# Starting 24 of 71 expert blocks early, from a table of their own, and sending six results inside the last dispatch

## The chip, the cores and the metric

One core of one Trainium2 chip. The metric is the device time of one execution in microseconds (us), as the median of several; the profile shows one execution, with times from the start of its span.

## What the kernel computes

The reference is a one-layer model over 8 sequences of 512 tokens, with 192 features per token:

```python
h = tok(x, quantum_params, post_w, post_b)          # 6-qubit circuit per token, then a linear map to 192
h = h + attention(layernorm(h), W_qkv, b_qkv)       # one head, softmax over 512 keys
h = h + experts(layernorm(h), Wg, W1, b1, W2, b2)   # 8 experts, the best 2 per token
```

`experts` takes, for each token, the two experts with the largest gate scores, weighs their outputs (gelu of a 192 to 384 map, then 384 to 192) with a softmax over these two scores, and adds them up.

## The kernel before, in words

A token's features stay in a short form: 32 numbers (the six circuit values, the attention's weights over them, the shares), from which matrices worked out at the start give everything else. The 4096 tokens are 8 batches of 512, each 4 tiles of 128.

**Attention** runs as one pipeline over the batches, with the order of every engine written out by hand. For batch b TensorE (`pe`) makes scores in two orders (`both_scores`), VectorE (`dve`) takes row maxima, ScalarE (`act`) takes the exponentials, and then follow `context`, `merged`, `a_transpose`, `gram`, the choice of two experts (`route_and_root`), the place of each token among those of its expert (`ranks`, `slots`), the features scaled for the experts (`normed`) and the shares (`shares`, which need an exponential that ScalarE takes in `gap_exponent`). `residual` writes what a batch has before its experts into `hres`.

**Dispatch.** GpSimd (`pool`) sends each batch's rows to `routed` in DRAM with eight indirect DMAs (`scatter(b, 0)` and `scatter(b, 1)`, four each, 64 in all). Each expert has its own region of `routed`, in order of tokens.

**Expert blocks.** A block is 128 rows of one expert. There are at most `BLOCKS` = 71 blocks, in `STEPS` = 18 steps of four. `block_table` on VectorE works out, from the counts of all batches, where each block starts in `routed` and which expert's weights it needs (`t_i`). Blocks that hold rows of the first four batches alone come first: their first 24 are called `EARLY`. SyncE (`sp`) loads the 71 blocks one after the other, each with a register load from the table and then a DMA (lines 412 and 413): it first waits for `table_done`, then for the scatters of batches 0 to 3 (`scattered_early`), and before block 24 for those of batches 4 to 7 (`scattered_late`). For each step VectorE copies the up weights of its four blocks (`expert_up`, L1430); TensorE turns the four blocks (`block_transpose`, L1912), multiplies them with the up weights (`up_proj`, L1923) and then multiplies each with its down weights (`down_proj`, L1933, six matmuls); ScalarE takes the gelu (L1612) and multiplies with the share (`weighted`, L1624) into one of `RESULTS` = 8 result buffers. GpSimd sends each result to `shares_out` in DRAM (L696); before it sends result m it waits until result m - 4 has landed.

**End.** For each batch SyncE loads its two sums from `shares_out` (`load_sums`, L418) when enough results have landed: 39 for batches 0 to 3, then 47, 55, 63 and 71. VectorE adds them to `hres` (`add_experts`, L1417), and SyncE stores the batch (L422). SyncE takes load b + 1 before store b, all in one queue, behind the 71 block loads. On VectorE the additions stand in one order with the copies: `expert_up(14)`, additions of batch 0, `expert_up(15)`, batch 1, `expert_up(16)`, batch 2, `expert_up(17)`, batches 3 to 7.

Of the kernel before, what the change touches and what calls it, by code (L numbers as in the profile page):

```python
# [16 lines left out]
QUBITS = 6  # L17
# [14 lines left out]
def build(nc, token_ids, angles, emb_two, emb_raw, qkv_w, gate_w, up_w, down_w, out):  # L32
# [23 lines left out]
    RESULTS = 8  # L56
    LAG = 4
    ADDS_FROM = (2 * HALF * SEQ // P + E) // STEP + 4
# [24 lines left out]
    shares_out = nc.dram_tensor("shares_out", (2 * TOKENS, D), F32, kind="Internal").ap()  # L83
    shares_view = shares_out.rearrange("(k b p j) d -> b p k (j d)", k=2, b=BATCHES, j=TILES)
# [4 lines left out]
    with ctx:  # L89
# [7 lines left out]
        theta_all = sb("theta_all", [P, T, ANGLES])  # L97
        angle_stages = sb("angle_stages", [P, 3, CT, ANGLES])
        turns, turned, folded = [angle_stages[:, i] for i in range(3)]
        sine = sb("sine", [P, 2, USED, CT])  # L100
        cosine = sb("cosine", [P, 2, USED, CT])
# [4 lines left out]
        bloch = table("bloch", QUBITS, 8)  # L106
# [3 lines left out]
        chain = table("chain", QUBITS, 16)  # L110
        chain_q = table("chain_q", 4, 2, 2, 2)
# [55 lines left out]
        own_row = sb("own_row", [P, 2])  # L167
# [10 lines left out]

        def behind(room, pattern, **sizes):
            size = int(np.prod(list(sizes.values())))  # L180
            room[1] += size
            return room[0][:, room[1] - size:room[1]].rearrange(pattern, **sizes)
# [54 lines left out]
        t_i = sb("t_i", [P, 2], I32)  # L237
        xt = sb("xt", [P, 1, P])
# [3 lines left out]
        y = behind(up_room_1, "p (n d) -> p n d", n=RESULTS, d=D)  # L242
        hid = behind(up_room_1, "p (n h) -> p n h", n=STEP, h=HID)
        expert_sums = [prob[:, :, :].rearrange("p j s -> p (j s)")[:, 0:2 * TILES * D].rearrange("p (k x) -> p k x", k=2),
# [88 lines left out]
        count_done = sem("count_done")  # L333
        table_done = sem("table_done")
        block_in = [sem(f"block_in{s}") for s in range(STEPS)]
# [13 lines left out]
        def blocks_of(s):  # L349
            return range(s * STEP, min(s * STEP + STEP, BLOCKS))  # L350

# [39 lines left out]
        def _(sp):  # L391
# [1609 lines left out]
```

## Time and profile before

| | us |
|---|---|
| median of 3 runs (313.16 to 313.82) | 313.63 |
| the profiled execution | 313.38 |
| its span | 311.7 |

The profiled execution is 1.68 us longer than its span; that part lies outside the profile. A row of the timeline gives the start, the length (of several instructions run together, from the first start to the last end), the engine, the line, the operation, what it writes and reads, and in brackets the engine's idle time before it. SPq is the queue in which SyncE issues DMAs; PEld is TensorE's loading of weights. PEclk is the clock granted to TensorE as a share of 2.4 GHz.

### The profile page before, as it was taken

The numbers are of one execution on the slowest core, as the hardware profiler recorded it, in microseconds if no ns is written. First come the engines' busy times: TensorE is split into PE (matmuls) and PEld (weight loads), VectorE is DVE, ScalarE is ACT, GpSimd is POOL, SyncE is SP. The second block draws the span as 40 slices with busy tenths as digits, with TensorE's granted clock in tenths as the row PEclk, the third lists the DMA queues.
The fourth block names the chain that finished last, engine by engine and source line by source line (L and its number), as shares of the span: only waits on it lengthen the run. The fifth ranks groups of instructions, "written<-read, shape, count | busy, mean of one in ns | idle before, by whom it ended". The sixth has DMA issues, their size and how long they took to land.

```text
span 311.7 us, 6161 instructions
## 1 busy us (share of the span) xinstructions
PE 223.4 (72%) x1551; PEld 151.6 (49%) x1551; DVE 176.3 (57%) x685; ACT 119.4 (38%) x283; POOL 209.1 (67%) x281
## 2 busy tenths in 40 slices
PE   0650995587838689776885627999999999999600
PEld 0540652232514335443543226887878888777400
DVE  4756999647899886858468732312222221655222
ACT  1002012426522403564322333655655656555300
POOL 5776975803996878777767773676766765767540
PEclk9999999555885655798555556999999999999955
DMA  7810007970000000000000011222222225798634
GB/s 178 242 20 12 1 7 261 344 291 3 0 0 2 9 9 15 13 16 14 13 13 13 14 30 32 68 92 88 82 81 91 68 84 150 271 331 274 209 84 187
DMA packets 24398, 28.90 MB, mean 93 GB/s; under 512 B 14890, under 2 KB 17825, under 8 KB 24171
## 3 DMA queue, kind: packets, MB, share of 16 engines
q1 hardware_dynamic: 17884, 20.56, 21.2%
q0 software_dynamic: 6480, 7.94, 8.3%
q8 instruction: 14, 0.23, 0.3%
q14 instruction: 20, 0.16, 0.2%
HBM read 13.54 MB, written 15.63 MB: 94 GB/s over the span
## 4 chain that ended last, share of the span: by engine, by line
PE 47%; DVE 23%; POOL 9%; issue 7%; DMA 6%; ACT 5%; SPq 2%; DVEq 0%; POOLq 0%; ACTq 0%
PE bank_b L1933 27%; PE bank_a L1923 5%; POOL theta_all L462 5%; PE bank_b L1736 4%; PE bank_a L1743 3%; DVE nmax L1116 3%; POOL rs L634 2%; PE bank_c L1755 2%; DMA shares_out<-up 2%; ACT prob L1481 2%; DMA angle_stages<-shares_out 2%; PE bank_a L1809 1%; POOL routed L645 1%; SPq L412 1%; DVE chain_q L811 1%
## 5 line engine op out<-in xcount | busy, mean ns | idle before, releaser
L696 POOL DMA_INDIRECT shares_out<-up x71 | 72.6, 1022 | 38.8 <-ACT up L1624 19.4
L1933 PE MATMUL bank_b<-wide,up 128*128 x426 | 85.7, 345 | 2.3 <-issue 1.5
L645 POOL DMA_INDIRECT routed<-rows,slot x64 | 62.4, 975 | 22.6 <-issue 18.8
L1933 PEld LDWEIGHTS bank_b<-wide,up 128*128 128x128 f32 x426 | 68.2, 191 | 16.9 <-issue 16.7
L1430 DVE COPY up<-wide 32x384 f32 x71 | 26.6, 374 | 63.2 <-PE bank_a L1923 35.2
L1624 ACT ACTIVATE up<-bank_b,up 128x192 f32<-128x192 f32 x71 | 29.8, 420 | 35.3 <-PE bank_b L1933 34.5
L462 POOL DMA_INDIRECT theta_all<-angles,ids x32 | 31.2, 976 | 10.8 <-issue 9.0
L1612 ACT ACTIVATE up<-bank_a 128x384 f32<-128x384 f32 x71 | 34.2, 485 | 11.1 <-PE bank_a L1923 10.6
L1743 PE MATMUL bank_a<-keys_t,wt 32*128 32x512 f32 x64 | 27.8, 955 | 4.7 <-DVE nmax L1116 3.0
L1736 PE MATMUL bank_b<-queries_t,keys_t 32*128 32x512 f32 x64 | 24.6, 849 | 6.3 <-ACT keys_t L1459 3.5
L1116 DVE TENSOR_REDUCE nmax<-bank_a 128x2 f32<-128x1024 f32 x16 | 19.5, 1220 | 11.3 <-PE bank_a L1743 11.3
L1481 ACT ACTIVATE prob<-bank_b 128x1024 f32<-128x1024 f32 x16 | 16.4, 1023 | 16.3 <-PE bank_b L1736 16.3
L1923 PE MATMUL bank_a<-xt,up 32*128 32x128 f32 x426 | 18.5, 305 | 0.4 <-ACT xt L1618 0.4
L1809 PE MATMUL bank_a<-m,a2t 32*128 32x192 f32 x64 | 14.0, 523 | 4.8 <-ACT hres L1489 2.7
L1923 PEld LDWEIGHTS bank_a<-xt,up 32*128 32x128 f32 x426 | 15.0, 201 | 4.7 <-issue 4.0
L1755 PE MATMUL bank_c<-prob,u 128*32 128x128 f32 x256 | 12.9, 366 | 0.9 <-ACT prob L1481 0.7
L1809 PEld LDWEIGHTS bank_a<-m,a2t 32*128 32x128 f32 x64 | 7.5, 273 | 11.8 <-issue 10.5
L1447 ACT ACTIVATE sine<-angle_stages 128x480 f32<-128x480 f32 (+2 forms) x3 | 2.4, 784 | 28.2 <-DVE angle_stages L767 28.2
L1417 DVE TENSOR_TENSOR hres<-hres,prob 128x384 f32<-128x384 f32 x12 | 6.2, 554 | 10.8 <-DMA prob<-shares_out 10.7
L1755 PEld LDWEIGHTS bank_c<-prob,u 128*32 128x32 f32 x256 | 9.5, 146 | 5.0 <-ACT prob L1481 2.3
L1489 ACT COPY hres<-bank_a 128x384 f32<-128x384 f32 x16 | 7.6, 477 | 10.6 <-PE bank_a L1809 10.6
L1736 PEld LDWEIGHTS bank_b<-queries_t,keys_t 32*128 32x128 f32 x64 | 7.0, 251 | 9.1 <-issue 7.8
(399 smaller groups left out, 361.5 us busy)
## 6 DMA issues: line engine op xcount, KB each, us to landing
routed<-pad_rows SPq DMA_DIRECT2D x8, 528.0 KB, 5.2
out<-hres SPq DMA_DIRECT2D x8, 384.0 KB
wide<-down_w SPq DMA_DIRECT2D x1, 2304.0 KB, 11.7
prob<-shares_out SPq DMA_DIRECT2D x3, 768.0 KB, 4.8
angle_stages<-shares_out SPq DMA_DIRECT2D x3, 768.0 KB, 6.5
up<-up_w SPq DMA_DIRECT2D x1, 1536.0 KB
form_p<-shares_out SPq DMA_DIRECT2D x2, 768.0 KB
up<-routed SPq DMA_DIRECT2D x71, 16.0 KB, 1.7
```

Source lines behind the costliest of these rows:

```text
L462: pool.indirect_dma_start(out=theta_all[:, t, :], out_offset=None, in_=angles, in_offset=bass.IndirectOffsetOnAxis(ids[:, b, j:j + 1], 0)) ...
L645: pool.indirect_dma_start(out=routed, out_offset=bass.IndirectOffsetOnAxis(slot[:, b, k, j:j + 1], 0), in_=rows[:, b, k, j, :], in_offset=None
L696: pool.indirect_dma_start(out=shares_out, out_offset=bass.IndirectOffsetOnAxis(xb[:, m, DEST:DEST + 1].bitcast(I32), 0), in_=y[:, m % RESU ...
L1116: dve.tensor_reduce(nmax[:, b % 2, 2 * h:2 * h + 2], bank_a[:, 0:2, :], AX.X, ALU.max, negate=True).then_inc(max_done, 1)
L1430: copied = dve.tensor_copy(up_now[r, s % 2, :], wide_flat[r, bass.ds(first + HC * D, HID)])
L1612: act.activation(hid[:, n, :], bank_a[:, n, 0:HID], ACT.Gelu).then_inc(gelu_done, 1)
L1624: act.mul(y[:, m % RESULTS, :], bank_b[:, m % 2, 0:D], xb[:, m, SHARE:SHARE + 1]).then_inc(y_done, 1)
L1736: mm = pe.matmul(bank_b[:, n, :], keys_t[r, bt % 3, k * P:(k + 1) * P], queries_t[r, :], start=True, stop=True)
L1743: mm = pe.matmul(bank_a[:, n, :], wt[r, bs % 2, :], keys_t[r, bs % 3, :], start=True, stop=True)
L1755: mm = pe.matmul(bank_c[j * F:(j + 1) * F, 0:P], u[:, b * TILES + k, :], prob[:, k, j * P:(j + 1) * P], start=(k == 0), stop=(k == TILES - 1),
L1923: mm = pe.matmul(bank_a[:, n, c * P:(c + 1) * P], up_now[r, s % 2, c * P:(c + 1) * P], xt[r, 0, :], start=True, stop=True)
L1933: mm = pe.matmul(bank_b[:, m % 2, 0:D], hid[:, m % STEP, c * P:(c + 1) * P], wide_flat[:, bass.ds(first + c * D, D)], start=(c == 0), stop ...
```

## The change

- **An early table.** With the counts of the first four batches (one more small matmul in `ranks(3)`, one more copy in `slots(3)`) VectorE works out the table of the first 24 blocks by itself (`early_table`, behind the last row maxima). It holds the rows in `routed`, the down weights and the up weights of each block.
- **Up weights by DMA.** SyncE writes all up weights once to `up_rows` in DRAM, long before. For the first 24 blocks (6 steps) it then loads, in addition to each block, that block's up weights from there, with a register load of its own. VectorE copies up weights from step 6 on only.
- **The order on SyncE.** It waits for `early_done` and the early scatters, issues four blocks and four up weights for each of the six steps, and then waits for `table_done` and the late scatters and issues the other 47 blocks.
- **The order on TensorE and ScalarE.** The expert steps start behind the last score products. The rest of the attention stage (`context(7)`, `merged`, `a_transpose`, `gram`, `ranks(6)` and `ranks(7)`) stands between the first expert operations. The residuals of batches 4 to 7 follow in pieces behind blocks 8 to 28, on other banks, and ScalarE copies each half in two pieces. The counts for the whole table move into `ranks(7)`; `block_table` moves ahead of `shares(7)`. The gelu is no longer touched in advance.
- **Results.** 24 result buffers in place of 8 (they lie where the circuit's tables were). GpSimd sends the first six results between `scatter(7, 0)` and `scatter(7, 1)`.

The core of the diff:

```diff
-    RESULTS = 8
+    RESULTS = 24
+    EARLY_STEPS = EARLY // STEP
+    TAIL_FIRST = 2 * STEP
+    TAIL_PIECES = 3 * (BATCHES - HALF) - 1
     LAG = 4
+    AHEAD = 6
...
+            sp.wait_ge(up_copied, E)
+            sp.dma_start(up_rows.rearrange("(e f) h -> f e h", f=F), wide[0:F, :, HC * D:WIDE]).then_inc(up_out, 16)
+
+            def load_up(m):
+                row = sp.value_load(t_early[m:m + 1, 2:3], min_val=0, max_val=(E - 1) * F)
+                n = m % STEP
+                sp.dma_start(up_early[m // STEP][n * F:(n + 1) * F, :], up_rows[bass.ds(row, F), :]
+                             ).then_inc(early_up_in[m // STEP], 16)
+
             def load_block(m):
-                row = sp.value_load(t_i[m:m + 1, 0:1], min_val=0, max_val=ROWS - P)
+                row = sp.value_load(table_of(m)[m:m + 1, 0:1], min_val=0, max_val=ROWS - P)
...
+            sp.wait_ge(early_done, 1)
+            sp.wait_ge(up_out, 16)
+            sp.wait_ge(scattered_early, 16 * 2 * TILES * HALF)
+            for s in range(EARLY_STEPS):
+                for m in blocks_of(s):
+                    load_block(m)
+                for m in blocks_of(s):
+                    load_up(m)
             sp.wait_ge(table_done, 1)
-            sp.wait_ge(scattered_early, 16 * 2 * TILES * HALF)
-            for m in range(EARLY):
-                load_block(m)
             sp.wait_ge(scattered_late, 16 * 2 * TILES * (BATCHES - HALF))
...
+                if b == BATCHES - 1:
+                    for m in range(AHEAD):
+                        result(m)
                 scatter(b, 1)
-            for m in range(BLOCKS):
...
+            for m in range(AHEAD, BLOCKS):
+                result(m)
...
                 normed(i - 2)
+                if i == BATCHES + 1:
+                    block_table()
                 shares(i - 2)
                 if i + 1 < BATCHES:
                     row_max(i + 1, 1)
                     spread_max(i + 1)
-
-            block_table()
+                    early_table()
...
-            for s in range(STEPS):
+            for s in range(EARLY_STEPS, STEPS):
                 expert_up(s)
...
+            xt_copy(0)
+            context_copy(BATCHES - 1)
+            at_copy(BATCHES - 1)
+            gap_exponent(BATCHES - 2)
             for m in range(STEP - 1):
                 gelu(m)
             xt_copy(1)
...
                 if m > 0:
                     weighted(m - 1)
+                    tail_copy(m - 1)
...
+                if m == 2:
+                    gap_exponent(BATCHES - 1)
...
-            residual(BATCHES - 1, 0)
-            residual(BATCHES - 1, 1)
-            pe.wait_ge(table_done, 1)
+            pe.wait_ge(early_done, 1)
             pe.wait_ge(down_in, 16)
-            pe.wait_ge(h2_copied, 2 * BATCHES)
             block_transpose(0)
+            context(BATCHES - 1)
             up_proj(0)
+            merged(BATCHES - 1)
+            a_transpose(BATCHES - 1)
+            ranks(BATCHES - 2)
+            gram(BATCHES - 1)
             block_transpose(1)
             for m in range(BLOCKS):
                 s, n = divmod(m, STEP)
+                if m == EARLY:
+                    pe.wait_ge(table_done, 1)
                 down_proj(m)
                 if n == 0 and s + 1 < STEPS:
                     up_proj(s + 1)
+                if m == 1:
+                    ranks(BATCHES - 1)
                 if n == 2 and s + 2 < STEPS:
                     block_transpose(s + 2)
+                tail(m)
```

## Rows read from the trace of the kernel before

**Rows 1.** The page's chain that ended last, shares of the span by engine
```profile
PE 47%; DVE 23%; POOL 9%; issue 7%; DMA 6%; ACT 5%; SPq 2%; DVEq 0%; POOLq 0%; ACTq 0%
```

**Rows 2.** Stretches of 4 us: busy time by engine, granted clock, DMA share
```profile
core 0: us, PE busy (x) PEld busy (x) DVE busy (x) ACT busy (x) POOL busy (x), PEclk, DMA share, GB/s
148.00:152.00 4.00, 4.00 (x42) 3.07 (x44) 2.84 (x26) 1.03 (x3) 3.06 (x4) 0.50 0.05 12
152.00:156.00 4.00, 2.82 (x17) 1.48 (x15) 0.96 (x7) 1.95 (x4) 2.88 (x3) 0.50 0.07 16
...
188.00:192.00 4.00, 3.24 (x15) 2.51 (x19) 0.74 (x3) 1.08 (x3) 0.91 (x1) 0.50 0.13 23
192.00:196.00 4.00, 4.00 (x42) 3.75 (x35) 1.05 (x3) 1.99 (x6) 1.45 (x2) 0.87 0.16 40
```

**Rows 3.** Timeline of SyncE's queue, from the first block load to the end
```profile
178.54 82.33 SPq L413 DMA_DIRECT2D up<-routed  x71
260.99 0.39 SPq L418 DMA_DIRECT2D prob<-shares_out  x1
...
301.50 0.36 SPq L418 DMA_DIRECT2D angle_stages<-shares_out  x1
```

**Rows 4.** Median time of a DMA from issue to landing
```profile
up<-routed SPq DMA_DIRECT2D x71, 16.0 KB, 1.7
...
routed<-rows,slot POOLq DMA_INDIRECT x64, 2.1
```

**Rows 5.** Timeline of VectorE, end of the row maxima, start and end of `block_table`
```profile
147.59 0.18 DVE L1123 COPY w_rep<-nmax 128x16 f32<-128x16 f32 x1
...
173.69 0.16 DVE L1357 CAST count_i<-bank_a 128x8 int32<-128x8 f32 x1
...
177.40 0.16 DVE L1393 TENSOR_TENSOR t_i<-t_sum,own_row 128x2 int32<-128x2 f32 x1
```

**Rows 6.** Timeline of GpSimd: dispatch, first and last results
```profile
145.69 0.95 POOL L645 DMA_INDIRECT routed<-rows,slot  x1 [0.30 <-issue]
...
179.07 0.96 POOL L645 DMA_INDIRECT routed<-rows,slot  x1 [0.31 <-issue]
...
187.94 0.97 POOL L645 DMA_INDIRECT routed<-rows,slot  x1 [0.30 <-issue]
192.78 1.00 POOL L696 DMA_INDIRECT shares_out<-up  x1 [3.88 <-ACT up L1624]
...
298.05 0.98 POOL L696 DMA_INDIRECT shares_out<-up  x1 [0.31 <-DMA shares_out<-up]
299.33 0.98 POOL L696 DMA_INDIRECT shares_out<-up  x1 [0.30 <-issue]
```

**Rows 7.** Timeline of TensorE: first expert operations, `block_transpose(6)`, `up_proj(15)`, last blocks
```profile
189.24 2.29 PE L1933 MATMUL bank_b<-wide,up 128*128 x6 [0.47 <-issue]
191.45 1.67 PE L1923 MATMUL bank_a<-xt,up 32*128 32x128 f32 x24
...
217.88 0.27 PE L1912 MATMUL bank_d<-ident,up 128*128 128x128 f32 x1
...
272.66 0.95 PE L1923 MATMUL bank_a<-xt,up 32*128 32x128 f32 x24
...
286.19 7.01 PE L1933 MATMUL bank_b<-wide,up 128*128 x36
```

**Rows 8.** Timeline of VectorE: additions of batch 0, then the copies of step 15
```profile
265.83 2.09 DVE L1417 TENSOR_TENSOR hres<-hres,prob 128x384 f32<-128x384 f32 x4 [6.43 <-DMA prob<-shares_out]
...
270.23 0.46 DVE L1430 COPY up<-wide 32x384 f32 x1 [0.73 <-issue]
```

**Rows 9.** Timeline of ScalarE: the table for the gelu, and the last result
```profile
179.36 1.28 ACT L1629 ACT_TABLE_LOAD   x1
...
293.23 0.42 ACT L1624 ACTIVATE up<-bank_b,up 128x192 f32<-128x192 f32 x1 [0.73 <-PE bank_b L1933]
```

**Rows 10.** TensorE's matmuls of the residuals, by line
```profile
L1809 PE MATMUL bank_a<-m,a2t x64: 320/522/685, 122.4 to 178.3; 32*128 32x192 f32 x64
```

More of the change, by code:

```diff
@@ L109, in build @@
         step_m = table("step_m", QUBITS - 2, 8)
-        chain = table("chain", QUBITS, 16)
-        chain_q = table("chain_q", 4, 2, 2, 2)
+        chain = circuit_table(QUBITS, 16)
+        chain_q = circuit_table(4, 2, 2, 2)
         ends = table("ends", 6)
@@ L332, in build @@
         h2_out = sem("h2_out")
-        count_done = sem("count_done")
         table_done = sem("table_done")
+        early_done = sem("early_done")
+        up_out = sem("up_out")
+        early_up_in = [sem(f"early_up_in{s}") for s in range(EARLY_STEPS)]
         block_in = [sem(f"block_in{s}") for s in range(STEPS)]
@@ L350, in blocks_of, with table_of, tail_piece, tail_issued @@
             return range(s * STEP, min(s * STEP + STEP, BLOCKS))
+        def table_of(m):
+            return t_early if m < EARLY else t_i
+        def tail_piece(m):
+            k = 2 * ((m - TAIL_FIRST) // STEP) + m % STEP
+            return k + 1 if m >= TAIL_FIRST and m % STEP < 2 and k < TAIL_PIECES else None
+        def tail_issued(m):
+            done = [tail_piece(n) for n in range(m) if tail_piece(n) is not None]
+            turned = HALF + 1 + len([k for k in done if k % 3 == 0])
+            return turned, 2 * HALF + len(done) - (turned - HALF - 1)
         def blocks_until(b):
@@ L648, in scatter, with all_landed, result @@
                         ).then_inc(scattered_early if b < HALF else scattered_late, 16)
+            def all_landed(m):
+                pool.wait_ge(added[m % RESULTS], 16 * (m // RESULTS + 1))
+                pool.sem_inc(landed, 1)
+            def result(m):
+                pool.wait_ge(y_done, m + 1)
+                if m >= LAG:
+                    all_landed(m - LAG)
+                pool.indirect_dma_start(
+                    out=shares_out, out_offset=bass.IndirectOffsetOnAxis(xb[:, m, DEST:DEST + 1].bitcast(I32), 0),
+                    in_=y[:, m % RESULTS, :], in_offset=None, bounds_check=2 * TOKENS - 1,
+                    oob_is_err=False).then_inc(added[m % RESULTS], 16)
             def constants():
@@ L1810, in residual, with late_a2_transpose, late_residual, tail @@
                 mm.then_inc(h2_done, 1)
-            def counts():
-                pe.wait_ge(max_done, 2 * BATCHES)
-                for n, b in enumerate(ENDS):
-                    mm = pe.matmul(bank_a[:, 0, n * E:(n + 1) * E], ones_b[:, :], both[:, b, TILES, :], start=True,
-                                   stop=True)
-                mm.then_inc(count_done, 1)
+            def late_a2_transpose(b, m):
+                pe.wait_ge(gates_done, b + 1)
+                pe.wait_ge(xt_copied, m // STEP + 2)
+                pe.wait_ge(h2_copied, 2 * b)
+                pe.transpose(bank_d[:, 0:P], flat(ev, b), ident[:, :]).then_inc(a2t_done, 1)
+            def late_residual(b, h, m):
+                pe.wait_ge(table_done, 1)
+                pe.wait_ge(a2t_copied, b + 1)
+                pe.wait_ge(xt_copied, m // STEP + 2)
+                pe.wait_ge(h2_copied, 2 * b + h)
+                for n in range(2):
+                    r = slice((2 * h + n) * F, (2 * h + n + 1) * F)
+                    into = bank_c[:, 0:D] if n else bank_d[:, P:P + D]
+                    mm = pe.matmul(into, a2t[r, :], m2[r, :], start=True, stop=True)
+                mm.then_inc(h2_done, 1)
+            def tail(m):
+                k = tail_piece(m)
+                if k is not None:
+                    b, part = HALF + k // 3, k % 3
+                    if part == 0:
+                        late_a2_transpose(b, m)
+                    else:
+                        late_residual(b, part - 1, m)
             pe.wait_ge(weights_done, 3)
@@ L1875, in _ @@
             a2_transpose(1)
[L1877 to L1881 removed]
+            for i in range(LAST[0] + 1, BATCHES):
+                queries(i)
+                context(i - 1)
                 residual(i - 4, 0)
```

191 lines of the change are left out of this document (123 added, 68 removed).

## The prediction, made before the changed kernel was run

> **What bounds the kernel now.** I read the chain that ended last first: TensorE holds 47% of it, more than any other engine [rows 1]. Then the timelines from the middle to the end. The expert stage begins when the table is there: `block_table` ends at 177.56, and SyncE's first block load follows at 178.54 [rows 3, 5]. TensorE starts its first down product at 189.24 and its last ones end at 286.19 + 7.01 = 293.20 [rows 7]; in between it goes from step to step with nothing that waits for loads, since the last of the 71 loads is out by 260.87, 32 us ahead of its use [rows 3, 7]. GpSimd ends its dispatch at 187.94 + 0.97 = 188.91, waits 3.88 us for the first result and issues the last one at 299.33 [rows 6]. The end hangs on that: the last sum is loaded at 301.50, and 10.2 us later the span is over [rows 3]. So three runs stand beside each other: SyncE (71 loads, 178.54 to 260.87), TensorE (189 to 293) and GpSimd (120 to 300). An earlier start helps only as far as all three come along.
>
> **SyncE's queue, before and after.** Its loads come at (82.33 - 0.34) / 70 = 1.17 us from start to start, where 0.34 is about one DMA's own issue; the rest is the register load [rows 3]. No row shows a load of up weights, but it is the same pair, a register load and a DMA; I take 1.16, as in the early part, and bound it below by 1.11 (the pace of the first loads, my reading of the same timeline) and above by 1.5.
> - Start: the row maxima end at 147.77 [rows 5]. `early_table` has ten small operations; `block_table` has seventeen in 3.87 us, 0.23 each [rows 5]. So 147.77 + 2.3 = 150.1, and the first load 0.98 later (177.56 to 178.54), at 151.1. The early scatters are no hindrance: the 32nd of 64 is issued at 145.69 and lands 2.1 later [rows 4, 6].
> - The early stage: 48 loads, 151.1 + 48 x 1.16 = 206.8. Step s has its up weights at 151.1 + (8s + 7) x 1.16 + 1.7: step 0 at 160.9, step 5 at 207.3 (landing 1.7 [rows 4]). TensorE gets a step every 9.3 us.
> - The late 47 loads: the last starts at 206.8 + 46 x 1.17 = 260.6, and the first sum can be loaded at 261.1. Before it was 260.99. **The start moves 27.4 us forward, and the 24 added loads take 24 x 1.16 = 27.8 us of the same queue: for SyncE the early start is worth nothing.** What the change can save must come from the last 50.7 us, where before SyncE waited for results.
>
> **TensorE.** The parts of the attention stage that it now does between the first expert operations are moved, not removed; their cost lies under the 9.3 us per step, in which a step at full clock needs about 5.8 (from `block_transpose(6)` at 217.88 to `up_proj(15)` at 272.66 are 9.4 steps, 54.8 us [rows 7]). What holds TensorE is block 24: the load of block 27, step 6's last, is issued at 206.8 + 3 x 1.17 = 210.3 and landed at 212.0. So `block_transpose(6)` comes at 212.0 instead of 217.88: **5.9 us earlier, not 28**. From there on it runs as before. Behind blocks 20 to 28 stand four residual halves of two matmuls, 0.32 us at their shortest, and one transpose [rows 10]: 1.6 us by estimate, bounded by 0 (hidden behind weight loads) and 4. `up_proj(15)` would come at 212.0 + 54.8 + 1.6 = 268.4.
>
> **VectorE's order adds a wait.** `expert_up(15)` stands behind the additions of batch 0, and these wait for the first sum: 4.84 us after its issue before (260.99 to 265.83), and the four copies behind them end at 270.69 [rows 3, 8]. With the first sum at 261.1 they end at 270.8, so `up_proj(15)` waits 2.4 us, to 270.9. Behind it are step 16's and 17's copies, each behind one more addition of 2.09; they come in time. From `up_proj(15)` to the last product was 293.20 - 272.66 = 20.5; I take 20.0, since 16 more result buffers spare TensorE the short waits for a free one. End of TensorE: 290.9 instead of 293.2.
>
> **GpSimd.** A scatter takes (187.94 - 179.07) / 7 = 1.27 us, a result 1.28 [rows 6]. `scatter(7, 0)` is due at 179.07 and needs `shares(7)`, which now stands behind `block_table` (3.87) and behind `ranks(7)`, which TensorE reaches only after `down_proj(1)`. At half clock that is 160.9 + about 13.5 (gelu's table 1.28 [rows 9], three products of 2.3 and 1.7 [rows 7], and the rest of the attention) = 174.5; with 2.9 for slots, features and shares, 181.2. So GpSimd stalls 3 us. Then four scatters, six results (7.7) and four scatters: 199.9. The late scatters land at 202, before SyncE asks for them at 206.8, so this delay costs nothing; if the loads came faster it would. The floor of the other 65 results is 199.9 + 65 x 1.28 = 283.1, under TensorE's 290.9, so the six early results are not on the path either: GpSimd does the same 135 DMAs and catches up with TensorE.
>
> **The sum.** Last product 290.9, its share 0.42 [rows 9], last result issued by 291.5, last sum 2.17 later as before (299.33 to 301.50), at 293.7, and 10.2 to the end: 303.9. The gain is mostly the backlog of GpSimd: before it issued its last result 6.1 us after TensorE's last product, held up by the landing of results while the sums were loaded. With more buffers the backlog can lie longer, so I keep some of it, and some DMA time: 304 for the span, which with the 1.68 outside gives 305.7, from a profiled execution of 313.38 (0.25 below the median, which I neglect). **I forecast 305.5 us**, own range 301 to 309.
>
> **Rivals.**
> - *The loads come faster than 1.16.* The Trainium skill ("DMA: Bandwidth & Descriptors", Issuing engines are not separate DMA queues) says that the sequencer's time to initiate a DMA is usually small beside the DMA. Here rows 3 and 4 say otherwise, 1.17 against 1.7 us. By that rule the queue would hardly count. As a mechanism of this kernel: at 1.11 the late loads start at 204.4, `block_transpose(6)` comes at 209.5, the first sum at 256.5; TensorE ends some 4.5 earlier, 299.5 for the span, 301 us. Its floor is GpSimd's: 283.1 + 1.28 + 2.17 + 10.2 = 296.7 for the span, 298.4 us. Chance 0.20.
> - *Landing takes over.* From 261 the loads of sums run without a wait for results, beside 19 results, each of which waits for the fourth before it. If these go at 2.0 us apiece, as against 1.28 undisturbed, the last is issued at 261.1 + 19 x 2.0 = 299.1; 311.5 for the span at worst, half of that excess more likely, 308 to 311 us. Chance 0.15.
> - *No change: a load of up weights is dearer.* At 1.5 us (24 x 0.34 = 8.2 more) the first sum and block 24 come 8.2 later and all the gain is gone, 313.5 us. Nothing in the profile speaks for it but that no row shows it. Chance 0.07.
> - *Slower: TensorE at half clock.* The granted clock is 0.50 from 148 to 192, through a stretch in which TensorE is busy 2.82 of 4 us, and even through one of 4.00; it is up only in the stretch of 192 to 196, in the unbroken run that starts at 189.24 [rows 2, 7]. The early stage has gaps, a step every 9.3 us. The skill ("TensorE: Matmul & The Clock Gate", Part 1: The HAM clock gate) states that the throttled clock is the default and activity releases it; the trace agrees with it. If the clock stayed at half through the six early steps, a down product would take 2.29, an up projection 1.67 and a transpose about 0.5 [rows 7]. From 168.2, where the first product starts, nineteen, five and five of them end at 222.6, 10.6 after the 212.0 above, and five more products lose another 5.7; less the wait of 2.4 that this swallows, the end moves by 13.9, to some 319 us. It decides from a delay of about 10 us over the six steps on. Against it: at 4 x 2.29 + 1.67 + 0.5 = 11.3 per step of 9.3 TensorE would have no gap left, and an unbroken run is what brought the clock up. Chance 0.08.
>
> **How the numbers follow.** Forecast 0.50, faster loads 0.20, landing 0.15, dearer loads 0.07, half clock 0.08. A measurement of this kernel can tell about 0.2%, 0.6 us, from no change. Faster: 0.50 + 0.20 + 0.15 = 0.85; same 0.03 and slower 0.04 share the dearer loads; slower with the clock 0.12. The range of 298 to 312 takes in the first three cases and leaves out the last two and a little.
>
> **What would show it.** SyncE: 48 loads from about 151, the last of 95 near 260.6, the first sum near 261. TensorE: `up_proj(0)` near 161, steps 9.3 us apart until `block_transpose(6)` at 212, steps of 5.8 behind it, a wait before `up_proj(15)`. GpSimd: a stall of 3 us before `scatter(7, 0)`, six results, the dispatch over at 200, and its last result within 1 or 2 us of TensorE's last product. It would be wrong if the loads of up weights kept another pace than the blocks', if the clock fell in the early stage and TensorE got behind its loads, or if results and sums hindered each other more than before.

## The result, and the profile after

The changed kernel takes 310.74 us (median of 20 runs, 307.78 to 314.07), the kernel before 312.86 us on the same chip (20 runs, 309.77 to 315.40). The ratio is 0.9933 with a 95% interval of 0.9904 to 0.9961: 0.7% faster, where the forecast was 305.5 us, 2.6% faster, with an own range of 301 to 309. Medians here are of all runs and ratios of those within about 1.5% of their kernel's fastest, so that a ratio is not always the quotient of two medians. The profiled execution took 310.14 us, its span is 308.1 us.

The page's chain that ended last, shares by engine, to be set against [rows 1]:

```profile
SPq 27%; DVE 22%; PE 15%; issue 13%; POOL 9%; DMA 7%; ACT 5%; DVEq 1%; POOLq 0%; ACTq 0%
```

TensorE has lost the chain (15% against 47%), SyncE's queue has it. The timeline of that queue, from the first block load on, answers to [rows 3]:

```profile
150.81 4.05 SPq L458 DMA_DIRECT2D up<-routed  x4
155.63 3.59 SPq L453 DMA_DIRECT2D up<-up_rows  x4
160.41 3.71 SPq L458 DMA_DIRECT2D up<-routed  x4
...
200.90 3.65 SPq L453 DMA_DIRECT2D circuit<-up_rows  x4
205.39 54.13 SPq L458 DMA_DIRECT2D up<-routed  x47
259.64 0.39 SPq L463 DMA_DIRECT2D prob<-shares_out  x1
...
298.17 0.36 SPq L463 DMA_DIRECT2D angle_stages<-shares_out  x1
```

It starts 27.7 us earlier and loads its first sum 1.4 us earlier (259.64 against 260.99). TensorE, against [rows 7]; the two transposes are those of steps 6 and 7:

```profile
160.78 1.67 PE L2058 MATMUL bank_a<-xt,up 32*128 32x128 f32 x24
...
210.76 0.33 PE L2037 MATMUL bank_d<-ident,up 128*128 128x128 f32 x1
...
218.03 0.27 PE L2037 MATMUL bank_d<-ident,up 128*128 128x128 f32 x1
...
269.62 0.95 PE L2058 MATMUL bank_a<-xt,up 32*128 32x128 f32 x24 [0.36 <-DVE up L1515]
...
283.76 7.22 PE L2070 MATMUL bank_b<-wide,up 128*128 x36 [0.60 <-ACT up L1693]
```

The last product ends at 290.98 (293.20 before). GpSimd, against [rows 6]: the stall ahead of the last batch's first scatter, the dispatch's end, and the last results.

```profile
180.53 0.96 POOL L695 DMA_INDIRECT routed<-rows,slot  x1 [1.67 <-issue]
...
197.16 0.95 POOL L695 DMA_INDIRECT routed<-rows,slot  x1 [0.31 <-issue]
...
286.34 0.98 POOL L708 DMA_INDIRECT shares_out<-circuit,up  x1 [1.25 <-ACT circuit L1705]
289.32 1.37 POOL L708 DMA_INDIRECT shares_out<-circuit,up  x1 [2.00 <-ACT circuit L1705]
291.00 0.98 POOL L708 DMA_INDIRECT shares_out<-circuit,up  x1 [0.30 <-issue]
292.29 0.98 POOL L708 DMA_INDIRECT shares_out<-circuit,up  x1 [0.30 <-issue]
293.58 0.98 POOL L708 DMA_INDIRECT shares_out<-circuit,up  x1 [0.30 <-issue]
296.02 0.98 POOL L708 DMA_INDIRECT shares_out<-circuit,up  x1 [1.46 <-issue]
```

The last result leaves 5.0 us behind the last product (6.1 before). The end of the chain, in order of time (start, length, what), says what held it:

```profile
288.72 0.43 ACT circuit L1705
289.32 3.95 DMA shares_out<-circuit,up
293.58 0.98 POOL shares_out L708
294.56 0.72 issue
295.31 0.71 issue
296.02 2.08 DMA shares_out<-circuit,up
298.17 5.01 DMA angle_stages<-shares_out
```

The row to see is the second: a result's own transfer stands in the chain ahead of later results. GpSimd, before it issues result m, waits until result m - 4 has landed. The result of 289.32 is the fifth from the end, and the view of its tile gives it 5.9 us from issue to landing, not only the 3.95 of the chain; it landed at 295.2, and the last result, which waits for it, left at 296.02. The timeline names ScalarE for the waits at 286.34 and 289.32. For the first this is right: ScalarE ended that result at 285.46, 0.88 before, and 0.88 is also the distance at other waits for ScalarE (at 249.16, for instance). For the second it is not: ScalarE had ended at 286.62, 2.70 before, and the landing came last. So the profiled span of 308.1 divides at the last product: 291.0 up to it, 17.1 behind it. Before it was 293.2 and 18.5.

### The profile page after: what moved, and what is told of

Its sections match the earlier page's. It is cut to its first block, busy times and chain, and to the rows that moved or that the text cites. A ratio compares the mean times of both kernels' runs of the same rounds, so it can differ in the third digit from the quotient of the medians.

```text
span 308.1 us, 6215 instructions
## 1 busy us (share of the span) xinstructions
PE 220.3 (72%) x1552; PEld 150.4 (49%) x1552; DVE 170.0 (55%) x675; ACT 121.3 (39%) x292; POOL 208.2 (68%) x281
## 4 chain that ended last, share of the span: by engine, by line
SPq 27%; DVE 22%; PE 15%; issue 13%; POOL 9%; DMA 7%; ACT 5%; DVEq 1%; POOLq 0%; ACTq 0%
SPq L457 11%; SPq L458 10%; PE bank_b L2070 5%; POOL circuit L512 5%; SPq L451 4%; PE bank_a L1835 3%; DVE nmax L1175 3%; SPq L453 3%; PE bank_b L1828 2%; POOL rs L684 2%; DMA shares_out<-circuit,up 2%; DMA angle_stages<-shares_out 2%; DMA prob<-shares_out 2%; POOL routed L695 1%; ACT prob L1566 1%
## 5 line engine op out<-in xcount | busy, mean ns | idle before, releaser
L708 POOL DMA_INDIRECT shares_out<-circuit,up x71 | 71.5, 1007 | 35.1 <-issue 17.3
L2070 PE MATMUL bank_b<-wide,up 128*128 x426 | 88.4, 350 | 6.0 <-ACT up L1693 1.8
L2070 PEld LDWEIGHTS bank_b<-wide,up 128*128 128x128 f32 x426 | 69.7, 195 | 22.1 <-issue 22.0
L1515 DVE COPY up<-wide 32x384 f32 x47 | 18.3, 389 | 65.9 <-PE bank_a L2058 49.7
L1705 ACT ACTIVATE circuit<-bank_b,up 128x192 f32<-128x192 f32 x71 | 29.9, 421 | 38.2 <-PE bank_b L2070 38.2
L512 POOL DMA_INDIRECT circuit<-angles,ids x32 | 31.2, 976 | 10.8 <-issue 9.0
L1532 ACT ACTIVATE circuit<-angle_stages 128x480 f32<-128x480 f32 (+2 forms) x3 | 2.3, 781 | 28.2 <-DVE angle_stages L823 28.2
L1502 DVE TENSOR_TENSOR hres<-hres,angle_stages 128x384 f32<-128x384 f32 x12 | 6.2, 555 | 8.5 <-DMA angle_stages<-shares_out 8.4
L1835 PEld LDWEIGHTS bank_a<-keys_t,wt 32*128 32x128 f32 x64 | 7.0, 261 | 7.4 <-issue 4.8
L1540 ACT COPY wide<-bank_a 128x384 f32<-128x384 f32 x8 | 3.8, 478 | 16.7 <-PE bank_a L1773 16.7
```

The source lines that it names most:

```text
L512: pool.indirect_dma_start(out=theta_all[:, t, :], out_offset=None, in_=angles, in_offset=bass.IndirectOffsetOnAxis(ids[:, b, j:j + 1], 0)) ...
L708: pool.indirect_dma_start(out=shares_out, out_offset=bass.IndirectOffsetOnAxis(xb[:, m, DEST:DEST + 1].bitcast(I32), 0), in_=y[:, m % RESU ...
L1705: act.mul(y[:, m % RESULTS, :], bank_b[:, m % 2, 0:D], xb[:, m, SHARE:SHARE + 1]).then_inc(y_done, 1)
L1835: mm = pe.matmul(bank_a[:, n, :], wt[r, bs % 2, :], keys_t[r, bs % 3, :], start=True, stop=True)
L2070: mm = pe.matmul(bank_b[:, m % 2, 0:D], hid[:, m % STEP, c * P:(c + 1) * P], wide_flat[:, bass.ds(first + c * D, D)], start=(c == 0), stop ...
```

## The experiments

Each kernel was timed several times in turn with the kernel before on the same chip, and a ratio is to those runs; the kernel that loads its sums last was run once. Ratios of different groups of runs compare less well than those of one group. The edits are to the changed kernel, but for one to the kernel before; cuts in them are marked with three dots. The "tail" is the time from the end of TensorE's last product to the end of the span.

**The six early results back behind the dispatch.**
```
-    AHEAD = 6
+    AHEAD = 0
```


> The first six results go behind the dispatch, as before; all else as in the changed kernel. First theory (the six early results are not on the path): the dispatch ends 7.7 us earlier, near 190.5, GpSimd still does the same 135 DMAs, TensorE's last product stays near 291 and the span within 1 us of 308.1. Rival (sending them early is what pays): the span grows by 3 us or more.

Measured: 312.05 us, ratio 0.9965 (0.9918 to 1.0011). In its profile the dispatch is over at 190.8, the first sum is loaded at 260.66, the last result leaves at 296.42: neither of these two moves by more than 1.1 us, and the span is 308.5. TensorE's last product, expected near 291, came at 292.86; the tail was shorter by 1.5. At the pace of this kernel the six results are not on the path.

**Twelve results between a result and the landing it waits for, instead of four.**
```
-    LAG = 4
+    LAG = 12
```


> GpSimd waits for the landing of result m - 12 instead of m - 4 before it sends result m. First theory (the last results are held by the landing of the fourth before them, 6.5 us each while sums are loaded): the last result is issued within 1.5 us of TensorE's last product, at about 292 instead of 296, the last sum is loaded at about 296 and the span is about 305 to 306. Rival (the DMA engines are full, so that results only queue there instead of on GpSimd): the last result is issued earlier but lands as late as before, last sum at 298 and span 307.5 to 308.5.

Measured: 313.55 us, ratio 1.0048 (1.0013 to 1.0084); the simple remedy fell. The last result did leave 1.3 us behind the last product (296.57 against 293.99 + 1.24). But GpSimd's wait is also the report on which SyncE loads sums, and it now comes eight results later:

```profile
296.69 0.36 SPq L463 DMA_DIRECT2D prob<-shares_out  x1
...
302.79 0.36 SPq L463 DMA_DIRECT2D angle_stages<-shares_out  x1
```

The sum before the last is loaded at 296.69, beside the last results, and these land late again: 302.79 for the last sum, 6.2 us behind the last result (2.2 in the changed kernel). The last sum and the span of 312.7 lie outside what either theory expected.

**No sum loaded before all 71 results have landed.** The additions stand behind all copies of VectorE.
```
-                sp.wait_ge(landed, blocks_until(b))
+                sp.wait_ge(landed, BLOCKS)
-    ADDS_FROM = (2 * HALF * SEQ // P + E) // STEP + 4
+    ADDS_FROM = STEPS
```


> No sum is loaded before all 71 results have landed, and the additions stand behind all copies of up weights. The whole is slower by the unhidden sums; the place of the last result is what counts. First theory (sums loaded beside results hold the results up): each result lands in about 2.4 us to the end, and the last one is issued within 1.5 us of the last product, near 291 to 292. Rival (results are late for another reason, a wait on ScalarE or the pace of GpSimd itself): the last result stays 4 to 5 us behind the last product.

The time, 332.29 us, is that of eight sums one after the other and says nothing; the stretch of the results does. TensorE's last products, GpSimd's last result and, under them, the median landing of results from 255 to 293:

```profile
282.99 6.93 PE L2070 MATMUL bank_b<-wide,up 128*128 x36
```
```profile
292.02 0.99 POOL L708 DMA_INDIRECT shares_out<-circuit,up  x1 [0.30 <-issue]
```
```profile
shares_out<-circuit,up POOLq DMA_INDIRECT x27, 2.3
```

The same for the changed kernel, from 255 to 310:

```profile
form_p<-shares_out SPq DMA_DIRECT2D x2, 768.0 KB, 6.9
shares_out<-circuit,up POOLq DMA_INDIRECT x26, 4.0
```

Without sums in flight a result lands in 2.3 us, and the last one leaves 2.1 us behind the last product (282.99 + 6.93 = 289.92); with them it takes 4.0 and the last one leaves 5.0 behind. So the sums' loads, and the stores of finished batches (384 KB each) that go with them, cost 2.9 us there, through GpSimd's wait. The 2.1 is more than the 1.5 that the first theory allowed, but far from the rival's 4 to 5.

**SyncE spared twelve register loads and DMAs.** VectorE copies the up weights of steps 3 to 5, as it does those of the later steps.
```
+    LOADED_UPS = 3
-                for m in blocks_of(s):
+                for m in blocks_of(s) if s < LOADED_UPS else ():
                     load_up(m)
...
-            for s in range(EARLY_STEPS, STEPS):
+            for s in range(LOADED_UPS, STEPS):
                 expert_up(s)
...
```


> Only steps 0 to 2 have their up weights loaded by SyncE; VectorE copies those of steps 3 to 5 from the full weights, behind shares(7), where it was idle. SyncE has 12 loads less. First theory (the loads of up weights take from SyncE's queue what the early start gives): the early stage is over on SyncE near 192, the late loads start when the late scatters have landed, near 199.5 instead of 205.4, the first sum comes near 253.5 instead of 259.6, TensorE's block_transpose(6) near 205, its last product some 4 to 5 us earlier, and the span some 4 us shorter, 304, or less if the end is held by landings. Rival (what bounds is behind SyncE: landing of results and sums): the first sum moves by 6 us, but the last result and the end by less than 1.

Measured: 304.93 us, ratio 0.9764 (0.9708 to 0.9820). The first sum is loaded at 256.34, the last product ends at 289.66. That is 1.3 us earlier for TensorE, not the 4 to 5 expected; the profiled span (304.6) is 3.5 shorter, and the other 2.2 lie in the tail (14.9). That the gain stops short of the theory's 253.5 for the first sum is seen in TensorE's row of step 6:

```profile
206.81 0.33 PE L2039 MATMUL bank_d<-ident,up 128*128 128x128 f32 x1 [2.41 <-DMA up<-routed]
207.66 3.66 PE L2071 MATMUL bank_b<-wide,up 128*128 x12 [0.52 <-issue]
```

It waits for a block whose rows the last scatter brings, and that one is issued at 198.07, behind the six results. Now they are on the path. The 3.66 us for twelve products, 2.37 in the changed kernel, is the lower clock: the granted clock is 0.57 from 208 to 212.

**The same with the six results behind the dispatch.** The diffs of the first and the fourth kernel together.

> The run with SyncE's loads of steps 3 to 5 given to VectorE, with the six results behind the dispatch again. Theory (with the short queue the dispatch ends later than SyncE, so the six results now cost): the late scatters land some 7 us sooner, SyncE's late run starts at about 171 to 173 us instead of 178.4, block_transpose(6) comes at about 203 without a wait and without the half clock behind it, the first sum is issued at 248 to 251, the span is 299 to 302 and the ratio to the run with the six ahead some 0.98 to 0.99. Rival (the end is held by the results' landing): TensorE gains up to 4 us, the last result still leaves over 2 us behind the last product, and the span stays within 1.5 us of 304.6.

Measured: 304.19 us, ratio 0.9718 (0.9673 to 0.9762). The dispatch ends at 189.1, step 6 starts at 203.68 without a wait, the first sum is loaded at 245.83, the last product ends at 283.00: TensorE gains 6.7 us on the kernel above, some 2 of them because step 6 keeps the full clock (6.6 us for the step, 8.6 above).

```profile
245.83 0.50 SPq L464 DMA_DIRECT2D prob<-shares_out  x1
```

The span gains 3.9, since the tail takes the rest: 17.7 us against 14.9. The ratios of the two kernels can't be told apart. Both theories had a part of it. The chain's end has the transfers of results in it again:

```profile
276.74 3.15 DMA shares_out<-circuit,up
...
280.61 4.85 DMA shares_out<-circuit,up
```

**GpSimd waits for no landing.** ScalarE waits for the transfer from its own buffer, SyncE for those of the sums that it loads.
```
-                if m >= LAG:
-                    all_landed(m - LAG)
...
-                    act.wait_ge(landed, m - RESULTS + 1)
+                    act.wait_ge(added[m % RESULTS], 16 * (m // RESULTS))
...
-                sp.wait_ge(landed, blocks_until(b))
+                done = blocks_until(b)
+                for m in range(max(done - RESULTS, blocks_until(b - 1) if b else 0), done):
+                    sp.wait_ge(added[m % RESULTS], 16 * (m // RESULTS + 1))
```


> The changed kernel, in which GpSimd waits for no landing: ScalarE (before it writes a result's buffer again) and SyncE (before it loads sums) wait for the results' transfers themselves. Theory (GpSimd's wait for the landing of the result four before paces the end): the results leave as they are made, the last one within 2.5 us of the last product (5.0 in the changed kernel), the last sum is loaded at 294 to 296 instead of 298.2, the span falls by 2 to 4 us, ratio to the kernel before 0.981 to 0.988. Rival (the transfers themselves are slow beside the loads of the sums, and whoever waits for them waits as long): the last result may leave earlier, but the last sum is loaded at 297 to 299 and the span stays at 307.5 to 308.5.

Measured: 309.75 us, ratio 0.9872 (0.9819 to 0.9924). The last result leaves 1.8 us behind the last product (293.35 + 1.24 = 294.59), as the theory says:

```profile
293.35 1.24 PE L2068 MATMUL bank_b<-wide,up 128*128 x6 [0.20 <-issue]
```
```profile
296.34 0.98 POOL L708 DMA_INDIRECT shares_out<-circuit,up  x1 [0.30 <-issue]
```

But the last product is 3.6 us later than in the changed kernel. So the last sum (298.57) and the span (308.4) are where the rival put them; from the last product to the last sum it is 4.0 us, against 7.2 in the changed kernel, as in the theory. Two things are seen ahead of the late product. The first sum is loaded 0.85 us behind the last block load (206.71 + 55.26 = 261.97, then 262.82), where the changed kernel has 0.12: SyncE now goes through 24 semaphores there. And step 6 runs in part at the lower clock (below).

**The residual pieces on three blocks of a step instead of two.**
```
-            k = 2 * ((m - TAIL_FIRST) // STEP) + m % STEP
-            return k + 1 if m >= TAIL_FIRST and m % STEP < 2 and k < TAIL_PIECES else None
+            k = 3 * ((m - TAIL_FIRST) // STEP) + min(m % STEP, 2)
+            return k + 1 if m >= TAIL_FIRST and m % STEP != 2 and k < TAIL_PIECES else None
...
```


> The changed kernel with the eleven residual pieces on three blocks of each step instead of two, so that the last is done with block 21 instead of block 28. Theory (the pieces lengthen the steps behind block 12, 6.3 to 6.9 us against 5.76, and this carries to the end): the last product comes 1 to 2 us earlier and the ratio falls by 0.003 to 0.006. Rival (the end is set by SyncE's first sum at 259.6, the additions and the copies behind it): TensorE is earlier in steps 9 and 10 only, waits that much longer at up_proj(15), and the last product stays within 0.5 us of 291.0.

Measured: 310.46 us, ratio 0.9908 (0.9871 to 0.9944), not to be told from the changed kernel. TensorE is 0.9 us earlier in step 14 and waits 0.92 instead of 0.36 at `up_proj(15)`; its last product ends at 290.84. The rival holds: the pieces are not what sets the end.

**All four parts: copies by VectorE, six results behind, pieces moved, no landing waited for by GpSimd.**

> The parts together: up weights of steps 3 to 5 copied by VectorE, the six results behind the dispatch, the pieces on three blocks of a step, and no wait for a landing on GpSimd. Theory (SyncE's queue, then the late scatters, then the landing of the results are the gates in this order): first sum at 247 to 251, last product at 283 to 287, last result within 2.5 us of it, span 295 to 300, ratio to the kernel before 0.945 to 0.96. Rival (another gate, VectorE with 24 copies more or the transfers of the sums, holds the end): the span stays at 302 to 304.6.

Measured: 300.45 us, ratio 0.9594 (0.9543 to 0.9645), span 298.5; the last product ends at 284.44, the last result leaves 1.9 us behind it.

**The same without the pieces.**

> Up weights of steps 3 to 5 copied by VectorE, the six results behind the dispatch, and no wait for a landing on GpSimd; the residual pieces as in the changed kernel. Theory (GpSimd's wait for the landing of the result four before holds the last results up, the pieces hardly count): last product at 282.5 to 284, last result within 2.5 us of it (5.4 with the wait), ratio to the kernel before 0.958 to 0.966, as with the pieces moved (0.9594). Rival (the pieces gave that gain): ratio 0.968 to 0.974, as with the wait (0.9718).

Measured: 301.16 us, ratio 0.9694 (0.9626 to 0.9761), span 297.3; last product 283.18, last result 2.0 behind it. By the profile the theory holds. The ratio lies in the rival's bounds (0.968 to 0.974) and not in the theory's (0.958 to 0.966), but its interval covers both, so it cannot decide on the pieces.

**The kernel before, with no landing waited for by GpSimd.** The same edit in the kernel before; its eight buffers stay.

> The kernel before, in which GpSimd waits for no landing: ScalarE and SyncE wait for the results' transfers themselves; its eight result buffers stay. Theory (the tail behind the last product is GpSimd's wait for the landing of the result four before, in the kernel before as in the changed one): the last result leaves within 2.5 us of the last product instead of 6.1, span 307.5 to 309.5, ratio 0.986 to 0.993; the change then keeps no more of its gain than TensorE's 2.2 us. Rival (with eight buffers whoever waits for them waits as long): ScalarE waits for its buffer, the last product moves to 294 to 297, the span stays within 1 us of 311.7.

Measured: 310.19 us, ratio 0.9954 (0.9910 to 0.9998), span 306.9. The last result leaves 1.6 us behind the last product (285.19 + 7.29 = 292.48) instead of 6.1:

```profile
285.19 7.29 PE L1931 MATMUL bank_b<-wide,up 128*128 x36 [0.25 <-issue]
```
```profile
294.12 1.35 POOL L696 DMA_INDIRECT shares_out<-up  x1 [0.30 <-issue]
```

So the backlog is not the change's: the kernel before had it already. The gain in time is smaller than expected (0.986 to 0.993) and than the span of the one profile promised.

**The changed kernel with both, no landing on GpSimd and the pieces moved.**

> The changed kernel, with no wait for a landing on GpSimd and the residual pieces on three blocks of a step. Theory (the profile with the direct waits alone was late in TensorE by a stretch at the lower clock, which is not in the edit): last product at 290 to 292, last result within 2.5 us of it, span 303.5 to 306, ratio to the kernel before 0.980 to 0.986. Rival (without the wait on GpSimd the results crowd the DMA engines sooner and TensorE gets its blocks later): last product at 293 to 295 again, span 307 to 308.5, ratio 0.986 to 0.992.

Measured: 309.21 us, ratio 0.9910 (0.9870 to 0.9950), span 305.8. Last product 291.90, last result 1.5 behind it; the span is where the theory put it; the ratio is in the rival's bounds (0.986 to 0.992), and not below that of the moved pieces with the wait (0.9908, another group of runs). SyncE's 24 semaphores cost 0.85 here too (205.93 + 54.42 = 260.35, then 261.20).

**Additions one step further back in VectorE's order.**
```
-    ADDS_FROM = (2 * HALF * SEQ // P + E) // STEP + 4
+    ADDS_FROM = (2 * HALF * SEQ // P + E) // STEP + 5
```


> The changed kernel with the additions of each batch one step further back in VectorE's order, so that the copies for up_proj(15) no longer stand behind those of batch 0. Theory (this order costs the 0.4 us that the profile shows before up_proj(15), not the 2.4 of the forecast): last product at 290.3 to 291.2, the span within 1.5 us of 308.1, ratio 0.991 to 0.998. Rival (the wait only shows as short since TensorE was late itself): the last product comes 1.5 to 2.5 us earlier and the ratio falls to 0.985 to 0.990.

Measured: 310.32 us, ratio 0.9965 (0.9924 to 1.0005), span 308.4, last product 292.29. Nothing is gained, so the order of additions and copies cost no 2.4 us. The last product missed the theory's 290.3 to 291.2 by 1.1; step 6 came 0.7 later in this execution.

**GpSimd waits for no landing in its last twelve results alone; SyncE for the last sixteen results itself, and the changed kernel beside it.**
```
-                if m >= LAG:
+                if LAG <= m < REPORTED + LAG:
                     all_landed(m - LAG)
...
-                sp.wait_ge(landed, blocks_until(b))
+                sp.wait_ge(landed, min(blocks_until(b), REPORTED))
+                for m in range(max(blocks_until(b - 1), REPORTED) if b else BLOCKS, blocks_until(b)):
+                    sp.wait_ge(added[m % RESULTS], 16 * (m // RESULTS + 1))
...
```
Here REPORTED is 55.

> The changed kernel, in which GpSimd waits for no landing in its last twelve results alone; SyncE waits for the last sixteen results itself, before the last two sums. Theory (the tail is GpSimd's wait, and the version with direct waits throughout lost part of what it gained to SyncE's 24 waits in front of the first sum, 0.85 us against 0.12): first sum at once behind the late loads, last product at 290 to 291.5, last result within 2.5 us of it, from the last product to the end of the span 13.8 to 14.6 (17.1 in the changed kernel), ratio to the kernel before 0.979 to 0.987, 0.007 to 0.011 under that of the changed kernel in the same call. Rival (the transfers hold the end, whoever waits): 16 to 17.5 us from the last product to the end, ratio within 0.004 of the changed kernel's.

> The changed kernel itself, beside the two others on the same chip: ratio to the kernel before 0.990 to 0.996 as on record. By both theories the same.

Measured: 308.20 us, ratio 0.9840 (0.9798 to 0.9881), and for the changed kernel beside it 310.43 us, 0.9899 (0.9854 to 0.9944). The difference, 0.006, is just under the 0.007 to 0.011 expected and past the rival's 0.004, though the two intervals overlap. The last result leaves 1.8 us behind the last product, the tail is 14.6, and the first sum follows 0.11 us behind the last block load. The last product, at 294.18, was 2.7 us later than expected, again with step 6 at the lower clock.

**The same with VectorE's copies and the six results behind the dispatch.**

> The same with the up weights of steps 3 to 5 copied by VectorE and the six results behind the dispatch. Theory: TensorE's last product at 282.5 to 284 as in the runs with these two parts, 13.8 to 14.6 from it to the end, span 296.5 to 298.5, ratio 0.955 to 0.967. Rival (as above): span 299.5 to 301.5, ratio 0.969 to 0.976.

Measured: 301.46 us, ratio 0.9652 (0.9607 to 0.9696), span 299.1, tail 14.4; against the kernel with the same parts and the wait (0.9718) 0.7% less, measured in another group of runs, and the intervals touch. The last product, at 284.67, is 0.7 later than expected, and the span 0.6 longer. This and the two other kernels that join these parts, 300.5 to 301.5 us, are the fastest found and can't be told apart.

From the end of TensorE's last product to the end of the span, worked out from each profile:

| GpSimd waits for result m - 4 to the end | us | does not | us |
|---|---|---|---|
| before | 18.5 | before, no wait | 14.4 |
| changed | 17.1 | changed, no wait | 13.8 |
| VectorE copies, six behind | 17.7 | the same, no wait | 14.1 |
| additions later | 16.1 | changed, none for the last twelve | 14.6 |
| pieces moved | 15.3 | pieces moved, no wait | 13.9 |
| VectorE copies | 14.9 | all four parts | 14.1 |
| six results behind | 15.6 | VectorE copies, six behind, none for the last twelve | 14.4 |

(The kernel that waits for result m - 12 has 17.4.) With the wait the tail varies from 14.9 to 18.5; without it, it is 13.8 to 14.6. That it varies with how the last sums fall among the last results is a reading of the timelines, not a test.

## Why the prediction was wrong

**Right: SyncE's queue.** First load 150.81 (151.1 forecast), late loads from 205.39 (206.8), first sum 259.64 (261.1); the 24 added loads did eat the 27 us of the early start. The kernel with VectorE's copies and the six results behind shows the price: twelve loads less, and its first sum comes 259.64 - 245.83 = 13.8 us earlier, 1.15 a load. With VectorE's copies alone the time is 1.7% less by the two ratios (0.9764 against 0.9933, intervals apart, different groups of runs). The Trainium skill ("DMA: Bandwidth & Descriptors", Issuing engines are not separate DMA queues) calls the time to initiate a DMA usually small beside the DMA. The trace agrees for the issue alone, 0.33 us (median of the block loads) beside 1.7 to the landing. The prediction set 1.17 us against that rule, but most of it is the register load ahead of each DMA, with what goes with it: in the chain the line that loads a block's register, 457, has 11% of the span, the line of the DMA, 458, 10%. So the rule gave the rival "the loads come faster" no support; the pace was 1.14 us in the early part and 1.17 in the late.

**TensorE's end: right by number, in part by luck.** `up_proj(0)` at 160.78 (161), step 6 at 210.76 (212.0), last product 290.98 (290.9). The terms between were mis-sized against each other. Steps 6 to 8 took 7.27, 6.67 and 6.55 us, where later ones take 5.85, 2.9 us for the pieces in all (1.6 forecast). The wait before `up_proj(15)` was 0.36 (2.4). From there to the end it took 290.98 - 269.62 = 21.4 us, not 20.0; before it was 20.5, so the added buffers spared nothing here. The experiments with moved pieces and with later additions show that neither sets the end by itself. The profiled execution was also an early one: in the profiles of two near kernels with the same loads and the wait (six results behind, additions later) the last product came at 292.9 and 292.3. The rival "half clock" did not come: the granted clock, 0.50 up to 160, was 0.96 from 172 to 184, 0.86 from 184 to 196 and 1.00 from there to 290.

**Right: GpSimd's dispatch.** Over at 198.1 (199.9), the stall 1.67 (3), the six results not on the path, as the first experiment shows, and on it as soon as the loads come faster, as the text said.

**Wrong: "last result issued by 291.5".** This is the step that failed. It left at 296.02, 5.0 us behind the last product and not 0.6, and 308.1 - 304 = 4.1 us of span is all of the profiled error: the tail was worked out as 13.0 us and is 17.1. The prediction saw the 6.1 us of backlog in the kernel before, and gave its end to the larger number of buffers. But buffers are ScalarE's limit. GpSimd's wait is for the landing of the result four before, and that number is the same in both kernels, as is what slows the landing, the loads of the sums. The kernel before without this wait (1.6 us behind the last product), the changed one without it (1.8) and the one without sums in flight (2.1) show it. They also show that some 3 us of the miss are the wait; the rest is there without it, since even then GpSimd issues the last result 1.2 to 1.3 us after ScalarE has ended it (294.12 against 292.94, 296.34 against 295.04), and the sum has hardly anything between the two. The rival "landing takes over" named the mechanism, at a chance of 0.15; with half of its excess the last result leaves at 295.3, and its 308 to 311 us hold. It should have been the forecast, since nothing in the change touches the four.

**What the wait is worth in time** is less than the profiles say: 0.5% in the kernel before (0.9954, 0.9910 to 0.9998); 0.6% in the changed one (0.9840 against 0.9899 beside it, intervals overlapping); nothing with the pieces moved (0.9908 and 0.9910, different groups). No version of the changed kernel that only drops the wait, with the pieces moved or not, came under 0.984, and the forecast was 0.974. In their profiles the tail is 13.8 to 14.6, but the last product comes at 291.9 to 294.6.

**What is open.** The forecast had a gain of 313.63 - 305.5 = 8.1 us; the medians show 2.1. Of the 6.0 between them, 4.1 are the tail of the profiled execution, 0.4 lie outside the span (310.14 - 308.1 = 2.04 instead of 1.68), and 0.5 the forecast had neglected or rounded. The last 1.1 are that the profiled execution is kinder to the change than the medians are: its own time is 3.2 us under that of the kernel before (310.14 against 313.38), the medians differ by 2.1. What makes TensorE end later in other executions is not settled. One thing that some had and this one had not is TensorE at the lower clock in step 6, in four profiles of the ten in which SyncE loads all early up weights, the changed kernel's second among them: 8.6 to 9.0 us for the step instead of 7.2 to 7.4. No run was made to show what this is worth in the median.

## What to carry to other kernels

An engine that issues transfers and also waits for them, in order and at a fixed distance, paces its stream by the landing time of the moment; count that distance, not the buffers. Move such a wait to whoever needs the data, but count the semaphores that this puts on a loaded queue, and don't delay a report that another engine waits for. And where work is started earlier by giving its loads to a queue that is already full, look for the engine with room: twelve loads given to VectorE were worth 1.7% here, the whole change 0.7%.

## What the runs showed of the hardware

- Transfers that SyncE issues slow those that GpSimd issues: GpSimd's results of 128 rows landed in 2.3 us (median) by themselves and in 4.0 beside SyncE's loads of 768 KB and stores of 384 KB. The Trainium skill ("DMA: Bandwidth & Descriptors", Issuing engines are not separate DMA queues) says that DMAs run on the same 16 DMA engines and interleave, whichever engine started them; the slower landing agrees with that.
- 24 semaphore waits in a row, for results that had landed long before, in place of one cost SyncE 0.85 - 0.12 = 0.73 us, some 0.03 each. In the kernel before without GpSimd's wait there are eight, and the gap ahead of the first sum is 0.37 (190.11 + 67.67 = 257.78, then 258.15), about the same for each.
- TensorE's clock can fall in the middle of the expert stage. Stretches of 4 us of the kernel without the wait in its last twelve results (columns as in [rows 2]), and TensorE's rows of step 6:

```profile
208.00:212.00 4.00, 2.50 (x13) 1.92 (x13) 0.00 (x0) 2.71 (x8) 3.09 (x4) 1.00 0.30 94
212.00:216.00 4.00, 3.32 (x13) 2.72 (x13) 0.00 (x0) 1.07 (x3) 2.83 (x4) 0.79 0.29 88
216.00:220.00 4.00, 3.89 (x39) 2.93 (x38) 0.70 (x2) 1.84 (x6) 1.56 (x2) 0.78 0.24 66
220.00:224.00 4.00, 3.85 (x23) 3.13 (x27) 0.71 (x2) 2.69 (x9) 1.97 (x2) 1.00 0.17 41
```
```profile
212.16 0.33 PE L2038 MATMUL bank_d<-ident,up 128*128 128x128 f32 x1 [1.34 <-DMA up<-routed]
213.01 3.27 PE L2071 MATMUL bank_b<-wide,up 128*128 x12 [0.52 <-issue]
216.21 1.66 PE L2059 MATMUL bank_a<-xt,up 32*128 32x128 f32 x24
```

The granted clock goes from 1.00 (2.4 GHz) to 0.79 and 0.78, part of each stretch at 1.2 GHz, after TensorE had waited 1.33 us for up weights and 1.34 for a block; the up projection takes 1.66 instead of 0.95 us, step 6 8.96 instead of 7.27. The changed kernel's profile kept 1.00 there with a wait of 1.51 and none for the block.
